# Second attention of a ViT tower: the low half of the probabilities moves from VectorE to GpSimd, ScalarE's high half becomes one operation, and the queues stand in another order

## The chip, the cores and the metric

The kernel runs on one core of a Trainium2 chip. A core has TensorE (PE, matrix products into PSUM), VectorE (DVE), ScalarE (ACT), GpSimd (POOL) and SyncE (SP, which issues DMAs); each works through its own queue in order, and queues meet at semaphores. The metric is the time of one execution on the device in microseconds, the median of several runs. Times inside the kernel come from one profiled execution.

## The reference

64 images go through five steps: patch embedding, a first attention, a first MLP, the second attention, a second MLP. The change is in the second attention. With its 196 patches an image is one frame, so both parts of the reference's formula are plain attention over all 197 tokens of 192 channels, with 12 heads of 64:

```python
def _L1_attn_ref(x, W_qkv, W_0):            # x: normalised tokens, 64 x 197 x 192
    def _mhsa(q, k, v, scale):
        s = jnp.einsum('ghid,ghjd->ghij', q, k) * scale
        a = jax.nn.softmax(s, axis=-1)
        return jnp.einsum('ghij,ghjd->ghid', a, v)
    ...
    qkv = (x @ W_qkv).reshape(b, t, dh, 3, h)
    ...
    out = jnp.concatenate((out_cls, out_sp), axis=2)
    out = jnp.transpose(out, (0, 2, 1, 3)).reshape(b, t, h * dh)
    return out @ W_0
h = h + _L1_attn_ref(_layernorm(h, axis=-1), L1_attn_W_qkv, L1_attn_W_0)
```

Everything is float32 there. The kernel computes such products with float16 pairs: a number is split into a high part (its rounding to float16) and a low part (the rest), and three of the four partial products are summed.

## The kernel before, in words

The residual `h` of all images stays in SBUF. `attention_1` handles one image in each round of a loop, written out for an even and an odd image. An image has 197 tokens, in two row blocks of 128 and 69 (index `c`), and six pairs of heads (`n`). Each engine has a list of steps, its order. A step has a letter and a number; an apostrophe means that it belongs to the next image (two: to the one after), a caret to the image before. The lists set each engine's order fully; nothing is scheduled at run time but the waits.

The steps of one image, in the order of the data:
- `n`: VectorE normalises the image (`normalise_twice`, L137 and L139: two instructions for each row block, SBUF to SBUF, float32).
- `x`: TensorE transposes it into a bank (L1266, L1267), ScalarE copies the high part (L1334), VectorE subtracts for the low part (L1402, tile `fp`).
- `q0` to `q5`, `v0` to `v3`: TensorE makes queries and keys of a pair (L1273, ten matmuls) or half of the values of a row block (L1280, five); ScalarE takes the high part (L1348, L1334), VectorE the low one (L1419, L1402). The steps `x`, `q`, `v` and `w` share two PSUM banks in turn (`JOBS`, `job_before`), so each waits until VectorE has emptied the bank of the job before the last.
- `s`: TensorE's scores of a pair (L1291). `m` of VectorE: their maxima (L1429). `e` of ScalarE: four exponentials with their sums (L1363, into `b_pr`, three buffers). `r`: VectorE's reciprocal of the sums (L1435). `p` of GpSimd: two multiplications by it, in `b_pr` (L1512).
- `h`: ScalarE's high part of the probabilities (L1334, `b_halves`, two instructions, one for each row block). `l`: their low part, a subtraction with two SBUF inputs, for each row block. Pairs 2 and 5 have it on GpSimd (L1497), the others on VectorE (L1402).
- SyncE transposes both halves by DMA (L1478). `m` of TensorE: probabilities times values (L1305). `o`: output in two halves (L1334, L1402). `w`: output projection (L1315) and VectorE's addition to `h` with its statistics (L1454, L1458); in odd images two row blocks more than in even ones. `k`: GpSimd lays aside the left-over tokens of odd images (L1505).

Exponential `n` needs low part `n - 3` finished, high part `n` needs the DMA of `n - 3`, reciprocal `n` needs multiplication `n - 2`.

Of the kernel before, what the change touches and what calls it, by code (L numbers as in the profile page):

```python
# [1084 lines left out]
def attention_1(nc, S, n_img):  # L1085
# [9 lines left out]
    VH = 2 * D  # L1095
    FLIP_ROWS = (P, TAIL + 11)
    QUERIES = sum(FLIP_ROWS)
    PE_ORDER = ("m5^^ v2 s5^ q5 w^^ s0 x' v3 m0^ s1 m1^ m2^ q0' s2 q1' q2' m3^ s3 "
                "v0' q3' m4^ s4 q4' v1'").split()
    ACT_ORDER = ("e2 v0' q3' o1^ e3 q4' h1 v1' o2^ h2 v2' e4 q5' e5 h3 h4 v3' x'' "  # L1100
                 "e0' o0 h5 q0'' e1' q1'' q2'' h0'").split()
    DVE_ORDER = ("v1 o2^^ v2 m5^ r4^ n' q5 w^^ r5^ l3^ m0 v3 x' l4^ r0 m1 q0' o0^ m2 "
                 "r1 q1' q2' l0 m3 v0' r2 q3' m4 o1^ r3 q4' l1").split()
    POOL_ORDER = ("p1 p2 l2 p3 k^ p4 p5 p0' l5").split()
    JOBS = [s for s in PE_ORDER if s[0] in "xqvw"]
    assert len(JOBS) % 2 == 0

# [27 lines left out]
    with ExitStack() as ctx:  # L1135
# [91 lines left out]
        with nc.Block() as block:  # L1227
# [101 lines left out]
            @block.scalar  # L1329
            def _(act):  # L1330
                norm_s(act)

                def copy(dst, src):
                    return nc.scalar.activation(dst, src, ACT.Copy)  # L1334

                def step(s, kind, n, img, like, odd):
                    if kind in "xqv":
                        k = job_bank(kind, n)
                        act.wait_ge(*made(s, img))
                    if kind == "x":  # L1340
                        if later(img):
                            act.wait_ge(q_ready, PAIRS * img)
                            act.wait_ge(v_ready, 4 * img)
                        copy(xt[:, 0:2], banks[:, k, 0:2 * SEQ].rearrange("p (h t) -> p h t", h=2)).then_inc(xt_hi, 1)
                    elif kind == "q":
                        if later(img):
                            act.wait_ge(ready, PAIRS * (img - 1) + n + 1)
                        nc.scalar.activation(qk[:, n, 0], banks[:, k, 0:2 * SEQ].rearrange("p (g t) -> p g t", g=2), ACT.Copy,  # L1348
                                             scale=QK_SCALE).then_inc(qk_hi, 1)
                    elif kind == "v":  # L1350
                        if n % 2 == 0 and later(PAIRS * (img - 2) + 3):
                            act.wait_ge(mixed, PAIRS * (img - 2) + 3 * (n // 2) + 3)
                        c, col = n % 2, (n // 2) * VH
                        copy(val[odd][0:ROWS[c], 0, c, col:col + VH], banks[0:ROWS[c], k, 0:VH]).then_inc(v_hi, 1)
                    elif kind == "e":
                        if later(PAIRS * img + n - 1):
                            act.wait_ge(inverted, PAIRS * img + n - 1)
                        if later(PAIRS * img + n - 2):
                            act.wait_ge(*low_made(img, n - 3, 1))
                        for e in range(2):  # L1360
                            act.wait_ge(max_made[e], PAIRS * img + n + 1)
                            for c in range(2):
                                last = nc.scalar.activation(pr[n % 3][0:ROWS[c], c, e, :], scores[n % 2][0:ROWS[c], e, c * SEQ:(c + 1) * SEQ],  # L1363
                                                            ACT.Exp, bias=nmx[n % 2][0:ROWS[c], c, e:e + 1],
                                                            accum_out=rsum[n % 2][0:ROWS[c], c, e:e + 1])
                            last.then_inc(freed[e], 1)
                        if isinstance(img, int) and img == n_img - 1 and n in (2, 3):
                            gather_left(n - 2)
                    elif kind == "h":
                        act.wait_ge(prob_made, PAIRS * img + n + 1)  # L1370
                        if later(PAIRS * img + n - 2):
                            act.wait_ge(*turned(img, n - 3))
                        for c in range(2):
                            copy(halves[n % 3][0:ROWS[c], c, 0, :, 0:SEQ], pr[n % 3][0:ROWS[c], c]).then_inc(high_made, 1)
                    elif kind == "o":
                        act.wait_ge(mixed, PAIRS * img + 2 * n + 2)
                        if n == 0 and later(img - odd):
                            act.wait_ge(w_ready, img - odd)
                        if n == 0 and odd and later(img - 1):
                            act.wait_ge(left_taken, img - 1)  # L1380
                        copy(ot[:, 0, 2 * n:2 * n + 2, own(odd)], bank_o[:, (odd + n) % 2, 0:2 * SEQ].rearrange("p (f t) -> p f t", f=2)).then_inc(ot_hi, 1)

                def gather_left(m):
                    pairs = range(n_img // 2)[m * LEFT_PAIRS:(m + 1) * LEFT_PAIRS]
                    act.wait_ge(left_taken, 2 * pairs[-1] + 2)
                    copy(gathered[m].rearrange("p k (i t) -> p k i t", t=REST),
                         ol[:, 2 * pairs[0] + 1:2 * pairs[-1] + 2:2, :].rearrange("p i (k t) -> p k i t", t=REST)).then_inc(left_gathered, 1)

                run(act, ACT_ORDER, step)
                gather_left(2)  # L1390

            @block.vector
            def _(dve):
# [10 lines left out]
                def step(s, kind, n, img, like, odd):  # L1404
# [26 lines left out]
                    elif kind == "r":  # L1431
                        if later(PAIRS * img + n - 1):
                            dve.wait_ge(prob_made, PAIRS * img + n - 1)
                        dve.wait_ge(freed[1], PAIRS * img + n + 1)
                        v.reciprocal(rinv[n % 2][:], rsum[n % 2][:]).then_inc(inverted, 1)  # L1435
                    elif kind == "l":
                        for c in range(2):
                            dve.wait_ge(high_made, 2 * (PAIRS * img + n) + c + 1)
                            low(halves[n % 3][0:ROWS[c], c, 1, :, 0:SEQ], pr[n % 3][0:ROWS[c], c],
                                halves[n % 3][0:ROWS[c], c, 0, :, 0:SEQ]).then_inc(low_by_v, 1)  # L1440
                    elif kind == "o":
                        dve.wait_ge(ot_hi, 3 * img + n + 1)
                        low(ot[:, 1, 2 * n:2 * n + 2, own(odd)], bank_o[:, (odd + n) % 2, 0:2 * SEQ].rearrange("p (f t) -> p f t", f=2),
                            ot[:, 0, 2 * n:2 * n + 2, own(odd)]).then_inc(ot_split, 1)
                    elif kind == "w":
                        if isinstance(img, int) and img == 0:
                            dve.wait_ge(moved, 16 * MOVES)
                        if isinstance(img, int) and img == n_img - 1:
                            add_left(0, banks[:, 1 - k, 0:D])
                            add_left(1, banks[:, 1 - k, D:2 * D])  # L1450
                        dve.wait_ge(*made(s, img))
                        tiles = ((img - 1, 1), (img, 0)) if odd else ((img, 0),)
                        for m, (i, c) in enumerate(tiles):
                            last = v.tensor_tensor(h[:, i, c, :], banks[:, k, m * D:(m + 1) * D], h[:, i, c, :], ALU.add)  # L1454
                        last.then_inc(h_updated, 1)
                        dve.wait_ge(h_updated, img + 1)
                        for i, c in tiles:
                            v.bn_stats(S["stats"][:, 2 * i + c, :], h[:, i, c, :])  # L1458
# [26 lines left out]
            @block.gpsimd  # L1485
            def _(pool):
                for r in range(3):
                    last = nc.gpsimd.memset(halves[r][:], 0.0)
                last.then_inc(cleared, 1)
                pool.wait_ge(cleared, 1)  # L1490
                pool.wait_ge(filled, 1)

                def step(s, kind, n, img, like, odd):
                    if kind == "l":
                        for c in range(2):
                            pool.wait_ge(high_made, 2 * (PAIRS * img + n) + c + 1)
                            nc.gpsimd.tensor_tensor(halves[n % 3][0:ROWS[c], c, 1, :, 0:SEQ], pr[n % 3][0:ROWS[c], c],  # L1497
                                                    halves[n % 3][0:ROWS[c], c, 0, :, 0:SEQ], ALU.subtract).then_inc(low_by_p, 1)
                        return
# [316 lines left out]
```

## Time and profile before

| | |
|---|---|
| three runs, median | 2526.62 us (2522.15 to 2528.86) |
| profiled execution | 2526.39 us, span of its instructions 2524.6 us |
| busy over the span | PE 2210.4 (88%), DVE 2187.8 (87%), ACT 2067.5 (82%), POOL 1362.8 (54%) |
| granted TensorE clock, mean | 0.971 |
| second attention | from about 790 to 2300 us |
| largest group | L1512 POOL `b_pr`, 768 instructions, 687.1 us busy |

The chain that ended last lies in the last stage only, so it says nothing of the second attention; there the windows, the waits and the timelines have to be read. In a timeline a row merges equal neighbours ("x2"); its duration runs from the first start to the last end. Neighbours overlap by 0.04 to 0.13 us, so what an instruction costs its engine is the difference of two starts, not its duration.

### The profile page before, as it was taken

How to read it: one execution, taken by the hardware profiler on the slowest of the kernel's cores; microseconds unless marked ns; L12 is line 12 of the kernel's file. 1: busy time of each engine (PE TensorE's matmuls, PEld its weight loads, DVE VectorE, ACT ScalarE, POOL GpSimd, SP SyncE). 2: the span in 40 equal slices, each digit the busy share in tenths (PEclk: the TensorE clock that was granted, in tenths of full speed). 3: DMA queues.
4: the chain of work that ended last, by engine and by line, in shares of the span. 5: the costliest groups of instructions: out<-in, count | busy, mean ns of one | idle time of the engine just before them, and what ended most of it. 6: DMA issues, size and time to landing. Idle time of an engine off the chain costs nothing. (4 is left out here: it accounts for less than half of the span.)

```text
span 2524.6 us, 77423 instructions
## 1 busy us (share of the span) xinstructions
PE 2210.4 (88%) x25422; PEld 1717.7 (68%) x25422; DVE 2187.8 (87%) x5350; ACT 2067.5 (82%) x6129; POOL 1362.8 (54%) x1778
## 2 busy tenths in 40 slices
PE   5899999999998888888888888888898888888876
PEld 5778876888786666666666666666666666665554
DVE  5776668888885999999999999999999999996876
ACT  4677776777773898889888988988898889886997
POOL 5777742333331566656565666666565666662322
PEclk9999999999999999999999999999999999997999
DMA  6344410001000765556555555655565556562111
GB/s 179 107 114 121 117 30 28 5 5 42 14 5 3 110 116 108 112 111 114 109 108 108 112 113 107 115 109 112 110 115 108 110 110 115 112 111 47 53 46 57
DMA packets 734157, 222.65 MB, mean 88 GB/s; under 512 B 667590, under 2 KB 732720, under 8 KB 733808
## 3 DMA queue, kind: packets, MB, share of 16 engines
q1 hardware_dynamic: 734064, 221.56, 42.9%
q8 instruction: 41, 0.67, 0.1%
q14 instruction: 52, 0.43, 0.1%
HBM read 46.49 MB, written 9.68 MB: 22 GB/s over the span
## 5 line engine op out<-in xcount | busy, mean ns | idle before, releaser
L1512 POOL TENSOR_TENSOR b_pr<-b_pr,fc 128x394 f32<-128x394 f32 (+1 forms) x768 | 687.1, 917 | 453.7 <-DVE fc L1435 453.5
L1363 ACT ACTIVATE b_pr<-b_scores,fc 128x197 f32<-128x197 f32 (+1 forms) x1536 | 632.1, 439 | 43.3 <-DVE fc L1429 42.2
L1273 PE MATMUL b_banks<-fp,wqkv 128*128 128x197 f16 x3840 | 392.0, 250 | 65.1 <-DVE fp L1402 47.7
L1273 PEld LDWEIGHTS b_banks<-fp,wqkv 128*128 128x128 f16 x3840 | 315.2, 98 | 127.7 <-DVE fp L1402 56.1
L1429 DVE TENSOR_REDUCE fc<-b_scores 128x2 f32<-128x394 f32 x768 | 396.0, 555 | 2.4 <-PE b_scores L1291 0.4
L1334 ACT ACTIVATE b_halves<-b_pr 128x394 f16<-128x394 f32 (+1 forms) x768 | 367.4, 548 | 3.6 <-DMA b_pt<-b_halves 0.9
L1402 DVE TENSOR_TENSOR b_halves<-b_pr,b_halves 128x394 f16<-128x394 f32 (+1 forms) x512 | 359.2, 743 | 3.6 <-ACT b_halves L1334 1.6
L1363 ACT ACTIVATION_READ_ACCUMULATOR b_pr<-b_scores,fc 128x1 f32 (+1 forms) x1536 | 338.9, 221 | 0.0
L1497 POOL TENSOR_TENSOR b_halves<-b_pr,b_halves 128x394 f16<-128x394 f32 (+1 forms) x256 | 227.8, 912 | 131.8 <-ACT b_halves L1334 131.8
L977 POOL TENSOR_TENSOR h<-h,fp_bias 69x192 f32 (+3 forms) x128 | 133.4, 1070 | 266.8 <-DVE m_xn L139 266.8
L1291 PE MATMUL b_scores<-b_qk 64*128 64x197 f16 (+1 forms) x4608 | 270.5, 251 | 5.7 <-ACT b_pr L1363 5.7
L1280 PE MATMUL b_banks<-wqkv,fp 128*128 128x384 f16 (+1 forms) x1280 | 263.0, 338 | 6.1 <-DVE b_qk L1419 2.2
L479 PE MATMUL tokens<-tok_w,parts 128*128 128x192 f16 (+1 forms) x2304 | 207.8, 251 | 49.9 <-POOL parts L338 49.9
L1291 PEld LDWEIGHTS b_scores<-b_qk 64*128 64x128 f16 (+1 forms) x4608 | 186.4, 104 | 78.8 <-issue 56.9
L479 PEld LDWEIGHTS tokens<-tok_w,parts 128*128 128x128 f16 (+1 forms) x2304 | 194.1, 108 | 60.2 <-POOL parts L338 40.6
L1334 ACT ACTIVATE b_val<-b_banks 128x384 f16<-128x384 f32 (+1 forms) x256 | 126.5, 494 | 111.2 <-PE b_banks L1280 111.2
L1419 DVE SCALAR_TENSOR_TENSOR b_qk<-b_banks,b_qk 128x394 f16<-128x394 f32 x384 | 205.3, 548 | 13.1 <-ACT b_qk L1348 12.9
L338 POOL TENSOR_TENSOR parts<-patches,parts 128x394 f16<-128x394 f32 x192 | 179.0, 962 | 51.5 <-ACT parts L381 51.5
L1348 ACT ACTIVATE b_qk<-b_banks 128x394 f16<-128x394 f32 x384 | 192.1, 507 | 11.5 <-PE b_banks L1273 9.1
L1077 PE MATMUL m_bank_y<-fp,m_hid 128*128 128x192 f16 (+1 forms) x2304 | 195.4, 246 | 1.3 <-DVE h L955 1.3
L1077 PEld LDWEIGHTS m_bank_y<-fp,m_hid 128*128 128x128 f16 (+1 forms) x2304 | 190.4, 105 | 1.7 <-issue 1.5
L1025 ACT ACTIVATE m_act<-m_bank_h,fc_bias 128x394 f32<-128x394 f32 x192 | 112.8, 588 | 87.1 <-PE m_bank_h L1066 75.2
(250 smaller groups left out, 4437.7 us busy)
## 6 DMA issues: line engine op xcount, KB each, us to landing
patches<-in_x SPq DMA_DIRECT2D x64, 588.0 KB, 4.3
b_pt<-b_halves SPq DMA_TRANSPOSE x384, 3.2
out<-z_res SPq DMA_DIRECT2D x64, 96.0 KB
fc<-b_halves SPq DMA_TRANSPOSE x192, 3.2
fp<-b_halves SPq DMA_TRANSPOSE x192, 3.2
m_raw_weights<-in_wqkv SPq DMA_DIRECT2D x2, 1152.0 KB, 6.9
out<-z_res SPq DMA_DIRECT2D x32, 51.8 KB
h<-h SPq DMA_DIRECT2D x32, 44.2 KB
```

Of the source, the lines that this page charges most:

```text
L479: last = t.matmul(tokens[m][0:ROWS[c], c * D:(c + 1) * D], parts[m][:, pa, k, COLS[c]], tok_w[:, pb, k, :], start=(k == 0 and n == 0), sto ...
L1077: last = t.matmul(bank_y[m][0:ROWS[c], c * D:(c + 1) * D], hid[b][:, pa, f, lo:lo + ROWS[c]], S["fp"][:, pb, f, :], start=(f == 0 and j == ...
L1273: last = t.matmul(out[:, g * SEQ:(g + 1) * SEQ], w[:, (2 * n + g) * P:(2 * n + g + 1) * P], x, start=(j == 0), stop=(j == 4))
L1280: last = t.matmul(out[0:ROWS[c], 0:VH], x[:, COLS[c]], w[:, col:col + VH], start=(j == 0), stop=(j == 4))
L1291: last = t.matmul(scores[n % 2][0:ROWS[c], e, c * SEQ:(c + 1) * SEQ], qk[rows, n, pa, 0, COLS[c]], qk[rows, n, pb, 1, :], start=(j == 0), ...
L1334: return nc.scalar.activation(dst, src, ACT.Copy)
L1363: last = nc.scalar.activation(pr[n % 3][0:ROWS[c], c, e, :], scores[n % 2][0:ROWS[c], e, c * SEQ:(c + 1) * SEQ], ACT.Exp, bias=nmx[n % 2][ ...
L1402: return v.tensor_tensor(dst, src, high, ALU.subtract)
L1419: v.scalar_tensor_tensor(out=qk[:, n, 1], in0=banks[:, k, 0:2 * SEQ].rearrange("p (g t) -> p g t", g=2), scalar=QK_SCALE, in1=qk[:, n, 0], ...
L1429: v.reduce_max(nmx[n % 2][:, :, e], scores[n % 2][:, e, 0:2 * SEQ].rearrange("p (c t) -> p c t", c=2), AX.X, negate=True).then_inc(max_mad ...
L1497: nc.gpsimd.tensor_tensor(halves[n % 3][0:ROWS[c], c, 1, :, 0:SEQ], pr[n % 3][0:ROWS[c], c], halves[n % 3][0:ROWS[c], c, 0, :, 0:SEQ], ALU ...
L1512: last = nc.gpsimd.tensor_tensor(p, p, inv, ALU.mult)
```

## The change

1. `POOL_ORDER` has `l` for all six pairs, `DVE_ORDER` none.
2. ScalarE's `h` is one instruction over both row blocks, 128 rows of 2 x 394 elements. For that the rows 69 to 127 of the second block of `b_pr` are set to zero once, at the start, by three GpSimd memsets, and ScalarE's first exponential waits for them. A low part waits for the whole high part, no longer for its row block's half.
3. All four orders are new. Among other things the next image's normalisation is made one image earlier (`n''`), behind reciprocal 4 and ahead of `w` and reciprocal 5.

```diff
-    PE_ORDER = ("m5^^ v2 s5^ q5 w^^ s0 x' v3 m0^ s1 m1^ m2^ q0' s2 q1' q2' m3^ s3 "
-                "v0' q3' m4^ s4 q4' v1'").split()
...
+    PE_ORDER = ("m0^ w^^ v3 s0 x' s1 m1^ m2^ q0' q1' s2 q2' v0' m3^ s3 q3' q4' m4^ "
+                "s4 v1' s5 m5^ q5' v2'").split()
+    ACT_ORDER = ("q2' h0 v0' e2 q3' e3 q4' h1 v1' o1^ o2^ h2 q5' v2' e4 e5 h3 v3' h4 "
+                 "x'' e0' h5 q0'' o0 q1'' e1'").split()
+    DVE_ORDER = ("m0 v3 x' m1 r0 q0' q1' m2 r1 o0^ q2' v0' m3 q3' r2 m4 q4' v1' r3 "
+                 "o1^ o2^ q5' v2' m5 r4 n'' w^ r5").split()
+    POOL_ORDER = ("l5^ l0 k^^ p1 p2 l1 l2 p3 p4 l3 p5 l4 p0'").split()
...
                     elif kind == "e":
+                        if isinstance(img, int) and img == 0 and n == 0:
+                            act.wait_ge(cleared, 1)
...
-                        for c in range(2):
-                            copy(halves[n % 3][0:ROWS[c], c, 0, :, 0:SEQ], pr[n % 3][0:ROWS[c], c]).then_inc(high_made, 1)
+                        copy(halves[n % 3][:, :, 0, :, 0:SEQ], pr[n % 3][:]).then_inc(high_made, 1)
...
                 for r in range(3):
+                    last = nc.gpsimd.memset(pr[r][:, 1], 0.0)
+                last.then_inc(cleared, 1)
+                for r in range(3):
                     last = nc.gpsimd.memset(halves[r][:], 0.0)
                 last.then_inc(cleared, 1)
...
                     if kind == "l":
+                        pool.wait_ge(high_made, PAIRS * img + n + 1)
                         for c in range(2):
-                            pool.wait_ge(high_made, 2 * (PAIRS * img + n) + c + 1)
```

VectorE before, from reciprocal 4 to low part 3, in the round ahead of the loop:

```order
L1435 RECIPROCAL fc<-fc 128x4
L137 TENSOR_SCALAR fc<-h,mean,rstd 128x128
L139 TENSOR_SCALAR fc<-h,mean,rstd 128x128
L137 TENSOR_SCALAR fc<-h,mean,rstd 69x128
L139 TENSOR_SCALAR fc<-h,mean,rstd 69x128
L1419 SCALAR_TENSOR_TENSOR b_qk<-b_banks,b_qk 128x394
L1454 TENSOR_TENSOR h<-b_banks,h 128x192
L1458 BN_STATS stats<-h 128x6
L1435 RECIPROCAL fc<-fc 128x4
L1402 TENSOR_TENSOR b_halves<-b_pr,b_halves 128x2x197
L1402 TENSOR_TENSOR b_halves<-b_pr,b_halves 69x2x197
```

VectorE now, the same place, from the maxima of pair 5 to reciprocal 5:

```order
L1430 TENSOR_REDUCE fc<-b_scores 128x2 x2
L1436 RECIPROCAL fc<-fc 128x4
L137 TENSOR_SCALAR fc<-h,mean,rstd 128x128
L139 TENSOR_SCALAR fc<-h,mean,rstd 128x128
L137 TENSOR_SCALAR fc<-h,mean,rstd 69x128
L139 TENSOR_SCALAR fc<-h,mean,rstd 69x128
L1455 TENSOR_TENSOR h<-b_banks,h 128x192
L1459 BN_STATS stats<-h 128x6
L1436 RECIPROCAL fc<-fc 128x4
```

The normalisation still stands between reciprocals 4 and 5, now of the image after the next; the low parts (`b_halves`) behind reciprocal 5 are gone, and a low part of queries and keys (`b_qk`) no longer stands between normalisation and addition.

GpSimd before, multiplications (`b_pr`, with the number of the buffer) 3, 4, 5 and 0 and the low part (`b_halves`) of pair 5:

```order
L1512 TENSOR_TENSOR b_pr0<-b_pr0,fc 128x394
L1512 TENSOR_TENSOR b_pr0<-b_pr0,fc 69x394
L1512 TENSOR_TENSOR b_pr1<-b_pr1,fc 128x394
L1512 TENSOR_TENSOR b_pr1<-b_pr1,fc 69x394
L1512 TENSOR_TENSOR b_pr2<-b_pr2,fc 128x394
L1512 TENSOR_TENSOR b_pr2<-b_pr2,fc 69x394
L1512 TENSOR_TENSOR b_pr0<-b_pr0,fc 128x394
L1512 TENSOR_TENSOR b_pr0<-b_pr0,fc 69x394
L1497 TENSOR_TENSOR b_halves2<-b_pr2,b_halves2 128x2x197
L1497 TENSOR_TENSOR b_halves2<-b_pr2,b_halves2 69x2x197
```

GpSimd now, from multiplication 3 to the low part of pair 4:

```order
L1516 TENSOR_TENSOR b_pr0<-b_pr0,fc 128x394
L1516 TENSOR_TENSOR b_pr0<-b_pr0,fc 69x394
L1516 TENSOR_TENSOR b_pr1<-b_pr1,fc 128x394
L1516 TENSOR_TENSOR b_pr1<-b_pr1,fc 69x394
L1501 TENSOR_TENSOR b_halves0<-b_pr0,b_halves0 128x2x197
L1501 TENSOR_TENSOR b_halves0<-b_pr0,b_halves0 69x2x197
L1516 TENSOR_TENSOR b_pr2<-b_pr2,fc 128x394
L1516 TENSOR_TENSOR b_pr2<-b_pr2,fc 69x394
L1501 TENSOR_TENSOR b_halves1<-b_pr1,b_halves1 128x2x197
L1501 TENSOR_TENSOR b_halves1<-b_pr1,b_halves1 69x2x197
```

Between two multiplications there is now a low part, and multiplication 5, which needs reciprocal 5, comes behind low part 3.

## Rows read from the trace of the kernel before

**Rows 1.** Window sums, 300 us of the second attention; stretch, length, busy by engine, PEclk, DMA.
```profile
1200.00:1500.00 300.00, 264.06 (x3306) 201.28 (x3306) 288.57 (x622) 265.40 (x958) 184.55 (x213) 0.97 0.58 110
```
**Rows 2.** Groups by shape, VectorE, 1200 to 2000 us; count, busy us, mean ns, idle.
```profile
L1402 DVE TENSOR_TENSOR b_halves<-b_pr,b_halves 69x394 f16<-69x394 f32 x139 | 123.1, 885 | 0.0
...
L1402 DVE TENSOR_TENSOR b_halves<-b_pr,b_halves 128x394 f16<-128x394 f32 x139 | 82.8, 596 | 1.1
...
L137 DVE TENSOR_SCALAR fc<-h,mean,rstd 128x128 f32 x34 | 43.5, 1278 | 4.1 <-issue 2.6
...
L1435 DVE RECIPROCAL fc<-fc 128x4 f32<-128x4 f32 x208 | 34.4, 165 | 4.8 <-ACT b_pr L1363 3.0
...
L137 DVE TENSOR_SCALAR fc<-h,mean,rstd 69x128 f32 x34 | 20.6, 605 | 0.0
```
**Rows 3.** Waits, 1200 to 2000 us: who waited for whom, us in total, times, longest.
```profile
POOL b_pr L1512 <- DVE fc L1435: 236.6, 105, 2.6
POOL b_halves L1497 <- ACT b_halves L1334: 69.3, 34, 2.2
...
PE b_banks L1266 <- DVE b_qk L1419: 59.0, 35, 2.5
ACT b_val L1334 <- PE b_banks L1280: 58.6, 35, 2.7
```
**Rows 4.** Timeline of VectorE: start, us, engine and operation, count, idle before.
```profile
1406.21 0.18 DVE L1435 RECIPROCAL fc<-fc 128x4 f32<-128x4 f32 x1 [0.17 <-ACT b_pr L1363]
1406.47 1.57 DVE L137 TENSOR_SCALAR fc<-h,mean,rstd 128x128 f32 x1
1407.96 0.88 DVE L139 TENSOR_SCALAR fc<-h,mean,rstd 128x128 f32 x1
1408.77 0.33 DVE L137 TENSOR_SCALAR fc<-h,mean,rstd 69x128 f32 x1
...
1409.28 0.55 DVE L1419 SCALAR_TENSOR_TENSOR b_qk<-b_banks,b_qk 128x394 f16<-128x394 f32 x1
1409.76 0.34 DVE L1454 TENSOR_TENSOR h<-b_banks,h 128x192 f32 x1
```
**Rows 5.** Timeline of GpSimd, from 1405 us.
```profile
1405.51 3.25 POOL L1512 TENSOR_TENSOR b_pr<-b_pr,fc 128x394 f32<-128x394 f32 x4
...
1417.20 1.78 POOL L1497 TENSOR_TENSOR b_halves<-b_pr,b_halves 128x394 f16<-128x394 f32 x2
1418.93 2.05 POOL L1512 TENSOR_TENSOR b_pr<-b_pr,fc 128x394 f32<-128x394 f32 x2
```
**Rows 6.** Timeline of ScalarE, from 1418 us.
```profile
1418.23 0.94 ACT L1348 ACTIVATE b_qk<-b_banks 128x394 f16<-128x394 f32 x2
1419.07 0.94 ACT L1334 ACTIVATE b_halves<-b_pr 128x394 f16<-128x394 f32 x2
1419.91 0.41 ACT L1363 ACTIVATE b_pr<-b_scores,fc 128x197 f32<-128x197 f32 x1
...
1421.51 0.49 ACT L1334 ACTIVATE b_val<-b_banks 128x384 f16<-128x384 f32 x1
1421.88 0.50 ACT L1348 ACTIVATE b_qk<-b_banks 128x394 f16<-128x394 f32 x1
1422.26 0.51 ACT L1334 ACTIVATE b_ot<-b_bank_o 128x394 f16<-128x394 f32 x1
```
**Rows 7.** Groups by shape, ScalarE, whole span; a wide copy of the first stage.
```profile
L381 ACT ACTIVATE parts<-patches 128x1182 f16<-128x1182 f32 x64 | 76.2, 1191 | 91.5 <-PE tokens L479 91.2 <-DMA patches<-in_x 0.2
```
**Rows 8.** Timeline of TensorE, from 1409 us.
```profile
1409.96 0.32 PE L1266 MATMUL b_banks<-ident,fc 128*128 128x128 f32 x1 [2.47 <-DVE b_qk L1419]
...
1410.36 1.03 PE L1280 MATMUL b_banks<-wqkv,fp 128*69 128x384 f16 x5
```
**Rows 9.** Window sums, columns as in rows 1.
```profile
1412.00:1414.00 2.00, 2.00 (x26) 1.40 (x22) 1.99 (x6) 1.45 (x7) 0.98 (x1) 0.50 0.77 148
```

More of the change, by code:

```diff
@@ L1097, in attention_1 @@
     QUERIES = sum(FLIP_ROWS)
-    PE_ORDER = ("m5^^ v2 s5^ q5 w^^ s0 x' v3 m0^ s1 m1^ m2^ q0' s2 q1' q2' m3^ s3 "
-                "v0' q3' m4^ s4 q4' v1'").split()
[L1100 to L1104, printed above, removed]
+    PE_ORDER = ("m0^ w^^ v3 s0 x' s1 m1^ m2^ q0' q1' s2 q2' v0' m3^ s3 q3' q4' m4^ "
[5 more added lines that the diff above has]
+    POOL_ORDER = ("l5^ l0 k^^ p1 p2 l1 l2 p3 p4 l3 p5 l4 p0'").split()
     JOBS = [s for s in PE_ORDER if s[0] in "xqvw"]
@@ L1436, in step @@
                     elif kind == "l":
+                        dve.wait_ge(high_made, PAIRS * img + n + 1)
                         for c in range(2):
-                            dve.wait_ge(high_made, 2 * (PAIRS * img + n) + c + 1)
                             low(halves[n % 3][0:ROWS[c], c, 1, :, 0:SEQ], pr[n % 3][0:ROWS[c], c],
@@ L1487, in _ @@
                 for r in range(3):
+                    last = nc.gpsimd.memset(pr[r][:, 1], 0.0)
+                last.then_inc(cleared, 1)
+                for r in range(3):
                     last = nc.gpsimd.memset(halves[r][:], 0.0)
                 last.then_inc(cleared, 1)
-                pool.wait_ge(cleared, 1)
+                pool.wait_ge(cleared, 2)
                 pool.wait_ge(filled, 1)
```

## Prediction

> **What bounds the kernel now.** I read the window sums first, to see which engine has no room in the second attention. There VectorE (DVE) is busy 96% of the time, ScalarE (ACT) and TensorE (PE) 88%, GpSimd (POOL) 62% [rows 1]. Then the groups by shape, for counts: 208 reciprocals, one for each pair of heads, in 800 us are 34.67 images, so one image takes 23.08 us [rows 2]. Then the waits: GpSimd is idle 236.6 us until a reciprocal of VectorE and 69.3 us until a high part of ScalarE, ScalarE 58.6 us until TensorE's value product, TensorE 59.0 us until VectorE has emptied a bank for the next image's transposes [rows 3]. All of them end, directly or one step on, at VectorE's queue. So an image costs what VectorE's queue costs: 288.57 / 300 x 23.08 = 22.2 us of work and 0.9 of idle time.
>
> Last the timelines, to see why VectorE's instructions are long. A low part of the probabilities should take 0.48 us for each of its two instructions; it takes 596 and 885 ns in the mean [rows 2]. The normalisation of the next image is four instructions, of which the first and third take 1278 and 605 ns in the mean, though one alone can take 0.33 [rows 2, 4]. Set the two timelines side by side. GpSimd ran four multiplications back to back from 1405.51 to 1408.76, at a pace of 0.80 ((3.25 - 0.04) / 4), so the second ended at 1407.15 and the third at 1407.95. VectorE's normalising instruction of 1406.47 ended at 1408.04, the next at 1408.84: each about 0.08 us behind the end of a GpSimd instruction. Once GpSimd had stopped, the last two took 1408.77 to 1409.28 = 0.51 together [rows 4, 5]. So whatever of VectorE reads only SBUF queues behind GpSimd, the first of a block even past two ends.
>
> **What is removed.** Four of six low parts leave VectorE: 139 of each shape in 34.67 images, so four pairs an image, (82.8 + 123.1) / 34.67 = 5.9 us by busy time, some 5.3 from start to start, since neighbours overlap by 0.08 [rows 2]. VectorE's sum falls from 22.2 to 16.9, plus what normalising gains below, so about 18. It is not the bound by its sum any more.
>
> **What GpSimd gets.** A multiplication pair takes 2 x 0.80 = 1.60; a low part 1417.20 to 1418.93 = 1.73 [rows 5]. Six of each are 20.0 us an image, with the copy of the left tokens 20.2. That is a floor: no less than 20.2 of 23.08.
>
> The Trainium skill (GPSIMD Engine Reference, section Key points) says VectorE is about twice as fast for elementwise work. By that rule alone the move is a loss: four pairs at 1.73 instead of 0.95 are 3.1 us more engine time an image. It decides only if GpSimd then is the last engine, which the sum above does not make it.
>
> **ScalarE's high part.** Two instructions take 1419.07 to 1419.91 = 0.84 now [rows 6]. The new one has 788 elements a row; the trace of this stage has none such. Bounds: not below one half (0.42), not above both (0.84). Between: 1182 elements of the same kind of copy take 1.191 us [rows 7], 394 take 0.52, so 0.85 ns an element and 0.86 for 788, less the 0.10 that neighbours overlap: 0.76. Taken: 0.76, a gain of 0.5 us an image. The price is that the low part waits for all of it, and not for its first half; that delay, 0.34, is hidden where GpSimd still multiplies.
>
> **The order.** Now find the chain that closes on itself. In the new queues the next image's normalisation stands behind reciprocal 4 and ahead of the residual addition and reciprocal 5 (the pieces of the order in the part on the change). TensorE's transposes need both: the normalised image, and the bank that the addition frees. ScalarE's copy of them heads the rest of its round. So a round is the path: ScalarE from that copy to exponential 4; VectorE from reciprocal 4 over the normalisation to the addition; TensorE's transposes; back to ScalarE. Its legs:
>
> ScalarE: five exponentials at 1.60 (1419.91 to 1421.51) = 8.00; four high parts at 0.76 = 3.04; six query-key copies at 0.40 (between 0.42, two from 1418.23 to 1419.07, and 0.38, from 1421.88 to 1422.26) = 2.40; three value copies at 0.37 = 1.11; three output copies and the transposes' copy, all of 394 elements, at 0.38 = 1.52 [rows 6]. Sum 16.07. Exponential 5, two high parts and a value copy stand beside VectorE's leg: 1.60 + 1.52 + 0.37 = 3.5, less than that leg, so they cost nothing; they would if it fell below 3.5.
>
> VectorE and TensorE: reciprocal 4 and its hand-overs 0.26 (1406.21 to 1406.47). Normalisation: between 3.2 (four ends of GpSimd at 0.80) and 3.9 (first 1.49, then three at 0.80), since GpSimd now has work queued all the while: it is in multiplications 3 and 4 and low part 3; I take 3.6, for it will at times wait for a high part. Before it was 2.81. The addition 0.34, two of them in odd images, mean 0.47; hand-over 0.13 (1409.83 to 1409.96); transposes 0.40 and their tail, 0.60; hand-over 0.10 [rows 4, 8]. Sum 0.26 + 3.6 + 0.47 + 0.13 + 0.60 + 0.10 = 5.16.
>
> ScalarE's waits inside its leg: now it is idle 34.6 us of 300, 2.7 an image [rows 1], 1.7 of it for the value product [rows 3], which in the new order lies outside the leg. That leaves 1.0; bounds 0 and 2.7. I take 1.1, because four operations of the new order (query-key copies 0 and 1, output copy 2, value copy 2) come straight behind the matmuls that make their input.
>
> An image: 16.07 + 5.16 + 1.1 = 22.33 us, 0.75 less than 23.08. Over 62 of 64 rounds, without filling and draining, 46 us. GpSimd is then busy 20.2 / 22.3 = 90%. The new memsets, three of half the width of the probabilities, stand ahead of the stage's first exponential; the first transposes, projections and maxima cover them. The profiled execution took 2526.39 (span 2524.6); the median of the runs is 2526.62, so both bases agree. 2526.4 - 46 = 2480.
>
> **A price of TensorE's clock.** TensorE stood idle 2.47 us before the transposes at 1409.96, and in the stretch from 1412 its granted clock was 0.50 [rows 8, 9]: 1.2 of 2.4 GHz. In the new order it waits at the same place, for VectorE. If all of transposes and the first projection ran at half clock in every image, the path would grow by 0.4 + 0.4; in the sum above this is left at what even images pay now.
>
> **Rivals.**
> First, normalising starves. For: the first instruction of a block already runs past one end of GpSimd that it could have used (1407.15) [rows 4, 5], and GpSimd has hardly a gap any more. Against: the second took exactly one end, and the last two none, with GpSimd at rest. If two more of the four skip an end, normalisation is 3.9 + 1.6 = 5.5, the image 24.2, 1.15 more than now: 62 x 1.15 = 71 and thus about 2598. The point from which it decides is a normalisation of 3.6 + 0.75 = 4.35 us. The Trainium skill (GPSIMD Engine Reference, section Key points) names this contention: GpSimd shares its SBUF interfaces with VectorE's two-port modes and two-SBUF-input instructions. The trace agrees, with 885 and 1278 ns [rows 2]; by that rule the low parts' half of it goes and the normalisation's stays.
> Second, GpSimd is the bound alone. Where GpSimd waits, normalisation takes 4 x 0.26 = 1.04 (0.51 for two [rows 4]) instead of 3.6, and the path falls to 19.8, below GpSimd's 20.2. With about 0.9 of remaining waits for high parts and reciprocal 5: 21.1 an image, 2.0 less, 2526 - 124 = 2402. Against: normalisation lies just where GpSimd has most queued.
> Third, the order eats the gain: ScalarE's waits inside its leg stay at 2.7 instead of 1.1: 16.07 + 5.16 + 2.7 = 23.9 at worst; half of the way there is 23.1, no change, 2526. For: five queues that hand over at many places; against: VectorE, which most waits ended at, has 4 us of room.
>
> **Chances.** Forecast 0.58, with a range of its own from 2450 to 2512 (normalisation 3.2 to 3.9, high part 0.72 to 0.84, waits 0.9 to 1.3). GpSimd alone 0.16. No change 0.09. Starved normalisation 0.17. The range of 8 in 10 cuts the far parts of the first and second rival: 2436 to 2545. A change below 0.3%, 7.6 us, can't be told from none; faster by more 0.75, same 0.09, slower 0.16.
>
> **What would show it.** The reciprocals' count in a window of this stage gives the image: 22.3. The four normalising groups should sum to some 3.6 from start to start; the high part one instruction of some 0.86; VectorE about 80% busy and GpSimd 90%; ScalarE's largest wait the one for the transposes (some 1.6 an image), and GpSimd's waits small. I am wrong if GpSimd's largest wait is still a reciprocal with several us an image, if the normalising mean passes 1.1 us an instruction, or if TensorE's clock falls in every image.

## The result: 2560.8 us, slower, and the profile after

The changed kernel takes 2560.81 us in the median (2560.11 to 2562.59), before 2527.71 in the same rounds: ratio 1.0136, 95% interval 1.0119 to 1.0154. I had forecast 2480.

The page of the changed kernel gives a span of 2558.2 us, and a granted clock of 0.947 against 0.971. The lost time lies in the second attention. Window sums (stretch, length, busy time of PE, weight loads, DVE, ACT and POOL with the number of instructions, PEclk, DMA), answering [rows 1]:

```profile
1200.00:1500.00 300.00, 262.48 (x3224) 207.03 (x3223) 243.59 (x509) 253.84 (x858) 258.01 (x312) 0.93 0.57 107
```

VectorE is down to 81% and GpSimd up to 86%, about as forecast; ScalarE has fallen to 85%, and the clock from 0.97 to 0.93. Groups by shape on VectorE, 1200 to 2000 us (count, busy us, mean ns), answering [rows 2]:

```profile
L137 DVE TENSOR_SCALAR fc<-h,mean,rstd 128x128 f32 x34 | 51.3, 1510 | 3.0
L139 DVE TENSOR_SCALAR fc<-h,mean,rstd 128x128 f32 x34 | 45.1, 1328 | 0.0
...
L1436 DVE RECIPROCAL fc<-fc 128x4 f32<-128x4 f32 x202 | 34.5, 171 | 11.5 <-ACT b_pr L1365 8.2
L137 DVE TENSOR_SCALAR fc<-h,mean,rstd 69x128 f32 x34 | 32.1, 943 | 0.0
L139 DVE TENSOR_SCALAR fc<-h,mean,rstd 69x128 f32 x34 | 21.2, 624 | 0.0
```

202 reciprocals where there were 208: 23.8 us an image by this count, against 23.08. The four normalising instructions sum to (51.3 + 45.1 + 32.1 + 21.2) / 34 = 4.4 us, 4.1 from start to start, where I had 3.6. The waits, answering [rows 3]:

```profile
PE b_banks L1266 <- DVE h L1455: 90.3, 34, 3.4
...
ACT fp L1334 <- PE b_banks L1267: 77.6, 34, 2.7
POOL b_halves L1501 <- ACT b_halves L1334: 53.3, 33, 3.0
POOL b_pr L1516 <- DVE fc L1436: 52.3, 51, 1.6
ACT b_qk L1348 <- PE b_banks L1273: 39.9, 48, 2.0
```

GpSimd's waits have gone from 306 to 106 us. What waits now is TensorE, 90.3 us for the addition behind the normalisation, then ScalarE, 77.6 for the transposes (2.3 us a round, 1.6 forecast) and 39.9 for query-key products: the path of the forecast. VectorE, with a fifth of its time free, also waits 87.7 us for ScalarE's query-key high parts. One round of it, in the timelines of VectorE, GpSimd, TensorE and ScalarE (start, us, instruction, count, idle before), answering [rows 4 to 6] and [rows 8]:

```profile
1419.50 0.18 DVE L1436 RECIPROCAL fc<-fc 128x4 f32<-128x4 f32 x1
1419.77 1.55 DVE L137 TENSOR_SCALAR fc<-h,mean,rstd 128x128 f32 x1
1421.24 1.78 DVE L139 TENSOR_SCALAR fc<-h,mean,rstd 128x128 f32 x1
1422.94 0.92 DVE L137 TENSOR_SCALAR fc<-h,mean,rstd 69x128 f32 x1
1423.78 0.33 DVE L139 TENSOR_SCALAR fc<-h,mean,rstd 69x128 f32 x1
1424.04 0.34 DVE L1455 TENSOR_TENSOR h<-b_banks,h 128x192 f32 x1
...
1443.30 1.47 DVE L137 TENSOR_SCALAR fc<-h,mean,rstd 128x128 f32 x1
```
```profile
1418.80 3.25 POOL L1516 TENSOR_TENSOR b_pr<-b_pr,fc 128x394 f32<-128x394 f32 x4
1422.00 1.78 POOL L1501 TENSOR_TENSOR b_halves<-b_pr,b_halves 128x394 f16<-128x394 f32 x2
1425.07 1.64 POOL L1516 TENSOR_TENSOR b_pr<-b_pr,fc 128x394 f32<-128x394 f32 x2 [1.28 <-DVE fc L1436]
```
```profile
1420.43 0.69 PE L1291 MATMUL b_scores<-b_qk 64*128 64x197 f16 x12
1424.51 0.47 PE L1266 MATMUL b_banks<-ident,fc 128*128 128x128 f32 x1 [3.40 <-DVE h L1455]
1424.78 0.42 PE L1267 MATMUL b_banks<-ident,fc 128*128 128x128 f32 x1
1424.99 0.32 PE L1266 MATMUL b_banks<-ident,fc 69*128 69x69 f32 x1
1425.11 0.32 PE L1267 MATMUL b_banks<-ident,fc 69*128 69x69 f32 x1
1425.36 1.17 PE L1291 MATMUL b_scores<-b_qk 64*128 64x197 f16 x12
1426.46 1.21 PE L1305 MATMUL b_bank_o<-fp,b_val 128*64 128x197 f16 x12
1427.45 0.85 PE L1305 MATMUL b_bank_o<-b_pt,b_val 128*64 128x197 f16 x12
...
1430.06 0.69 PE L1291 MATMUL b_scores<-b_qk 64*128 64x197 f16 x12
```
```profile
1425.62 0.50 ACT L1334 ACTIVATE fp<-b_banks 128x394 f16<-128x394 f32 x1 [2.68 <-PE b_banks L1267]
...
1427.62 0.86 ACT L1334 ACTIVATE b_halves<-b_pr 128x788 f16<-128x788 f32 x1
1429.31 0.50 ACT L1348 ACTIVATE b_qk<-b_banks 128x394 f16<-128x394 f32 x1 [0.82 <-PE b_banks L1273]
```

GpSimd runs without a gap from 1418.80 to 1423.78. The first normalising instruction passes the end at 1420.4 and gets through at 1421.32; the second, 1.78 us long, also lets one end pass (1422.0); the third ends 0.08 behind GpSimd's last; only the fourth takes 0.33. Then TensorE, after 3.40 us idle, runs in this round its transposes and scores at half speed: the twelve score matmuls take 1.17 us, against 0.69 at 1430.06. So does the first product with the values (1.21), and the second in part (0.85; in experiment 2 they take 0.70 and 0.68). The clock in that stretch:

```profile
1424.00:1428.00 4.00, 3.49 (x38) 3.05 (x40) 3.62 (x11) 2.38 (x10) 2.93 (x4) 0.57 0.56 107
```

ScalarE gets the query-key product late and is idle 0.82 us more. From normalisation to normalisation: 4.74 to the transposes, 1.11 to ScalarE's copy, 17.68 to the next block, 23.53.

Not every round is like this one. TensorE's wait ahead of the transposes alternates between 1.9 and 3.4 us. In 10 of the 34 rounds between 1200 and 2000 us all that follows the wait runs at full speed, and from ScalarE's copy to the next block it takes 17.23 us. In the other 24 the half clock begins at the transposes or up to three groups of matmuls later, and the same leg takes 17.7 to 19.3 us. The longest have it through the next twenty query-key matmuls, which then take 3.1 us instead of 1.87.

### The profile page after: what moved, and what is told of

Read it like the earlier page. It is cut to its first block and busy times, and to the rows that moved or that the text cites. A ratio compares the mean times of both kernels' runs of the same rounds, so it can differ in the third digit from the quotient of the medians.

```text
span 2558.2 us, 76264 instructions
## 1 busy us (share of the span) xinstructions
PE 2243.8 (88%) x25422; PEld 1780.4 (70%) x25422; DVE 1979.2 (77%) x4838; ACT 2036.8 (80%) x5745; POOL 1749.3 (68%) x2293
## 5 line engine op out<-in xcount | busy, mean ns | idle before, releaser
L1501 POOL TENSOR_TENSOR b_halves<-b_pr,b_halves 128x394 f16<-128x394 f32 (+1 forms) x768 | 682.3, 910 | 116.6 <-ACT b_halves L1334 105.8
L1516 POOL TENSOR_TENSOR b_pr<-b_pr,fc 128x394 f32<-128x394 f32 (+1 forms) x768 | 626.0, 842 | 116.4 <-DVE fc L1436 116.4
L1273 PE MATMUL b_banks<-fp,wqkv 128*128 128x197 f16 x3840 | 406.2, 262 | 14.0 <-DVE fp L1403 12.7
L1273 PEld LDWEIGHTS b_banks<-fp,wqkv 128*128 128x128 f16 x3840 | 341.2, 103 | 66.3 <-DVE b_val L1403 15.8
L1420 DVE SCALAR_TENSOR_TENSOR b_qk<-b_banks,b_qk 128x394 f16<-128x394 f32 x384 | 217.2, 566 | 167.8 <-ACT b_qk L1348 167.8
L1334 ACT ACTIVATE b_halves<-b_pr 128x788 f16<-128x788 f32 x384 | 340.4, 886 | 3.2 <-POOL b_pr L1516 2.4
L1365 ACT ACTIVATION_READ_ACCUMULATOR b_pr<-b_scores,fc 128x1 f32 (+1 forms) x1536 | 330.2, 215 | 0.0
L1280 PE MATMUL b_banks<-wqkv,fp 128*128 128x384 f16 (+1 forms) x1280 | 251.5, 327 | 2.3 <-DVE b_val L1403 1.7
L1266 PE MATMUL b_banks<-ident,fc 128*128 128x128 f32 (+1 forms) x128 | 36.9, 308 | 168.6 <-DVE h L1455 162.4
L1403 DVE TENSOR_TENSOR b_val<-b_banks,b_val 128x384 f16<-128x384 f32 (+1 forms) x256 | 141.4, 552 | 54.3 <-ACT b_val L1334 54.3
```

Source lines behind the costliest of these rows:

```text
L1273: last = t.matmul(out[:, g * SEQ:(g + 1) * SEQ], w[:, (2 * n + g) * P:(2 * n + g + 1) * P], x, start=(j == 0), stop=(j == 4))
L1280: last = t.matmul(out[0:ROWS[c], 0:VH], x[:, COLS[c]], w[:, col:col + VH], start=(j == 0), stop=(j == 4))
L1420: v.scalar_tensor_tensor(out=qk[:, n, 1], in0=banks[:, k, 0:2 * SEQ].rearrange("p (g t) -> p g t", g=2), scalar=QK_SCALE, in1=qk[:, n, 0], ...
L1516: last = nc.gpsimd.tensor_tensor(p, p, inv, ALU.mult)
```

## The experiments

Times are medians, ratios against the kernel before of the same rounds. "Image" is 800 us divided by a sixth of the reciprocals counted in it; legs are means of the starts over all rounds between 1200 and 2000 us.

### 1. Normalisation ahead of reciprocal 4

```diff
-    DVE_ORDER = "... m5 r4 n'' w^ r5"
+    DVE_ORDER = "... m5 n'' r4 w^ r5"
```

> The changed kernel with one step moved in VectorE's order: the normalisation n'' stands ahead of reciprocal 4, not behind it. Theory A (a round is the closed path normalisation, transposes, ScalarE's copy of them, five exponentials, normalisation): it starts some 0.5 us earlier, and since GpSimd then has no reciprocal 4 to go on with, it meets one multiplication pair only and takes 2.2 to 2.8 us instead of 4.1. The image falls from 23.6 to 21.8 to 22.3 us: 2440 to 2480 us. Theory B (GpSimd at 86% is the bound, so each wait of GpSimd costs): GpSimd now waits some 1.5 us more for reciprocal 4, the image grows to 24.5 or more: 2600 us and above.

Measured: 2401.11 us, ratio 0.9504 (0.9483 to 0.9525), faster than both. Windows, VectorE, GpSimd:

```profile
1200.00:2000.00 800.00, 735.96 (x9673) 574.72 (x9670) 633.00 (x1519) 752.65 (x2579) 768.15 (x930) 1.00 0.65 121
```
```profile
1417.72 0.42 DVE L137 TENSOR_SCALAR fc<-h,mean,rstd 128x128 f32 x1
1418.07 0.88 DVE L139 TENSOR_SCALAR fc<-h,mean,rstd 128x128 f32 x1
1418.87 0.33 DVE L137 TENSOR_SCALAR fc<-h,mean,rstd 69x128 f32 x1
1419.13 0.33 DVE L139 TENSOR_SCALAR fc<-h,mean,rstd 69x128 f32 x1
1419.38 0.16 DVE L1436 RECIPROCAL fc<-fc 128x4 f32<-128x4 f32 x1
```
```profile
1417.22 1.65 POOL L1516 TENSOR_TENSOR b_pr<-b_pr,fc 128x394 f32<-128x394 f32 x2
1419.62 1.64 POOL L1516 TENSOR_TENSOR b_pr<-b_pr,fc 128x394 f32<-128x394 f32 x2 [0.76 <-DVE fc L1436]
```

GpSimd has one multiplication pair, then nothing until reciprocal 4; one normalising instruction waits, 0.88, the other three do not. The block is 1.66 us. GpSimd loses 0.76 there and is still 96% busy; the clock is 1.00. Theory A's path is right, but the time lies below its range, since the block and the clock gain more than it had: image 21.05 us. Theory B is out.

### 2. TensorE kept working ahead of the transposes

```diff
+                    if kind == "x":
+                        if later(PAIRS * (img - 1)):
+                            for e in range(2):
+                                pe.wait_ge(freed[e], PAIRS * (img - 1))
+                        work(12, scores[1][:, 0])
```

> The changed kernel with 12 added matmuls of 394 columns (some 2.0 us) in TensorE's idle time ahead of the next image's transposes, into a scores bank that is free by then; their result is not used. They add nothing to any other engine. Theory C (the half clock after the long idle time costs about 0.8 of the 1.3 us that the image came out above the forecast: transposes, scores and query-key matmuls at half speed, and ScalarE waiting for them): granted clock in the second attention from 0.93 to above 0.98, image 22.8 us, 2505 to 2520 us. Theory D (the clock is a companion, all is in the normalisation): the clock rises and the time stays within 8 us of 2561.

Measured: 2504.31 us, ratio 0.9910 (0.9890 to 0.9930).

```profile
1200.00:2000.00 800.00, 753.44 (x9422) 574.77 (x9423) 675.35 (x1414) 709.90 (x2403) 716.47 (x866) 1.00 0.60 113
```

Theory C holds: clock 1.00, 56 us gained, while the normalising groups keep their times (1491 and 1340 ns for the 128-row ones). ScalarE's leg falls from 18.11 to 17.23 us, the one from transposes to its copy from 0.86 to 0.74. ScalarE's wait for query-key products, 39.9 us in the changed kernel, is 9.0 here.

### 3. Half of the normalisation

```diff
-                            last = normalise_twice(...)
+                            if c == 0 or (isinstance(img, int) and img == 0):
+                                last = normalise_twice(...)
```

> The changed kernel without the normalisation of the second row block (two of four instructions, from the second image on; the output of those rows is of stale values). Theory A (closed path over the normalisation): the block shrinks from 4.09 to some 2.7 us, the image by 1.4 us or, with less idle time and so less half clock, up to 1.9: 2440 to 2475 us. Theory B (GpSimd is the bound): GpSimd has the same work, the time falls by 10 us at most: 2550 or above.

Measured: 2430.92 us, ratio 0.9618 (0.9600 to 0.9637). The block is 2.75 us to its last end instead of 4.17, the image 21.6, the clock 0.97: 2.1 us shorter for 1.4 us of block. Theory A has the direction and named less half clock as the reason for more than 1.4, but the time lies 9 us below its range. GpSimd had the same work, so theory B is out again.

### 4. The high part in two instructions

```diff
-                        copy(halves[n % 3][:, :, 0, :, 0:SEQ], pr[n % 3][:]).then_inc(high_made, 1)
+                        for c in range(2):
+                            copy(halves[n % 3][0:ROWS[c], c, 0, :, 0:SEQ], pr[n % 3][0:ROWS[c], c]).then_inc(high_made, 1)
```

> The changed kernel with ScalarE's high part again in two instructions, and the low part waiting for its row block's half, as before the change. Theory A: ScalarE's leg of the path has four high parts, 4 x 0.09 = 0.36 us more: 22 us more, 2575 to 2590. Theory E (the low part's wait for the whole high part is what costs: GpSimd waits 53 us in 800 for high parts): GpSimd's wait falls by about 0.4 us at each of its waiting places and the time falls, 2530 to 2545.

Measured: 2539.85 us, ratio 1.0054 (1.0034 to 1.0074), so 21 us faster than the changed kernel. Theory E has the size, my sign was wrong: in this order the fused high part costs. I can't say by which hand-over; the wait of GpSimd for high parts fell only from 53.3 to 41.3 us in 800, and the block and the clock moved as well (0.93 to 0.95). By legs, 0.25 of the 0.3 us that a round gets shorter lie between the block's start and ScalarE's copy. The block's first two instructions take 1179 and 1772 ns there, instead of 1510 and 1328.

### 5. The kernel before, only the low parts moved

```diff
-    DVE_ORDER = "... r5^ l3^ m0 v3 x' l4^ r0 ... q2' l0 m3 ... q4' l1"
-    POOL_ORDER = "p1 p2 l2 p3 k^ p4 p5 p0' l5"
+    DVE_ORDER = "... r5^ m0 v3 x' r0 ... q2' m3 ... q4'"
+    POOL_ORDER = "l5^ l0 p1 p2 l1 l2 p3 k^ p4 l3 p5 l4 p0'"
```

> The kernel before with only the low parts moved: all six on GpSimd, in the order l5^ l0 p1 p2 l1 l2 p3 k^ p4 l3 p5 l4 p0'; VectorE's other steps, TensorE's and ScalarE's order and the two-instruction high part as before. Theory A (VectorE loses 5.3 us of work, but its normalisation, behind reciprocal 4 and now beside a GpSimd that always has work queued, grows to some 4 us, and the orders written for two low parts on GpSimd make it wait for high parts): 2520 to 2580 us. Theory F (the move pays by itself, the reordering only spoils it): GpSimd above 90% busy, 2400 to 2450 us.

Measured: 2578.76 us, ratio 1.0203 (1.0182 to 1.0225). Normalising groups of 69 rows:

```profile
L139 DVE TENSOR_SCALAR fc<-h,mean,rstd 69x128 f32 x33 | 44.8, 1357 | 0.0
L137 DVE TENSOR_SCALAR fc<-h,mean,rstd 69x128 f32 x33 | 42.9, 1300 | 0.0
```

Before, L139 took 332 ns and L137 605: now GpSimd does not stop under them. The 128-row ones got shorter (905 and 589 ns, before 1278 and 882), and the whole block went from 2.87 to 3.93 us. The time is in theory A's range, at its upper end. Theory F is out: the move alone loses, and the new orders with the fused high part win back 18 us of it.

### 6. The kernel before, normalisation ahead of reciprocal 4

```diff
-    DVE_ORDER = "v1 o2^^ v2 m5^ r4^ n' q5 ..."
+    DVE_ORDER = "v1 o2^^ v2 m5^ n' r4^ q5 ..."
```

> The kernel before with one step moved: normalisation ahead of reciprocal 4 (m5^ n' r4^ instead of m5^ r4^ n'). Theory A (the place of the normalisation against the reciprocal that sets GpSimd off is what counts, whoever makes the low parts): the block falls from 2.79 to about 1.7 us; VectorE is 96% busy, so the image gets 0.8 to 1.1 us shorter: 2455 to 2480 us. Theory G (the gain in the changed kernel came from its closed path, which this kernel has not): reciprocal 4 is later, GpSimd and ScalarE behind it too, and the time is 2515 us or more.

Measured: 2472.93 us, ratio 0.9786 (0.9769 to 0.9804). Windows, and the group that was 1278 ns:

```profile
1200.00:2000.00 800.00, 710.47 (x9167) 542.07 (x9165) 779.61 (x1727) 736.95 (x2661) 506.78 (x593) 1.00 0.61 115
```
```profile
L137 DVE TENSOR_SCALAR fc<-h,mean,rstd 128x128 f32 x36 | 17.5, 485 | 0.0
```

Theory A, in its range. The same exchange of two steps gains 2.1% with the low parts on VectorE and 6.2% (2401 against 2561) with all of them on GpSimd. So all else of the change is worth 72 us (2473 to 2401) once the normalisation is out of GpSimd's way.

### 7. and 8. From experiment 1 on: high part split, and low part 4 back on VectorE

> The changed kernel with the normalisation ahead of reciprocal 4 (2401 us, GpSimd 96% busy, ScalarE 94%), and the high part again in two instructions with the low part waiting for its half. ScalarE gets 6 x 0.09 = 0.54 us more work an image. Theory H (here GpSimd is the bound and its 0.8 us of waits are for reciprocals): no gain from the earlier low part, and ScalarE's 94% rises to 97%: 2400 to 2425. Theory E (the earlier start of the low parts gains as in the changed kernel): 2380 to 2393.

> The changed kernel with the normalisation ahead of reciprocal 4, and pair 4's low part back on VectorE, behind the maxima of the next image's pair 1. GpSimd loses 1.73 us of 20.2 an image. Theory H (GpSimd's sum is the bound): ScalarE is next with 19.8 us of work, the image falls from 21.1 to some 20.4: 2355 to 2380 us. Theory I (low parts on VectorE and GpSimd's instructions hold each other up, 1.3 us instead of 0.95 for a pair and as much on GpSimd, and ScalarE's queue follows): 2395 to 2430 us.

The edits are that of experiment 4, and `m1 l4^ r0` in VectorE's order with `l4` taken out of GpSimd's. Measured: 2410.90 us, ratio 0.9549 (0.9531 to 0.9567), theory H; and 2400.60, ratio 0.9502 (0.9486 to 0.9518), the same as experiment 1. There GpSimd falls from 96% to 88%, ScalarE stays at 94%, and GpSimd's wait for reciprocals grows from 28.9 to 69.7 us in 800. So GpSimd's sum was not the bound of experiment 1 by itself. What is, stays open; ScalarE's queue, as full in both, is the nearest candidate. Theory I's time came out, but not its reason: VectorE's two instructions took 603 and 556 ns, GpSimd's multiplications 0.85 us at most between 1200 and 2000 us, and nothing but the waits grew.

### 9. Normalisation behind the addition

```diff
-    DVE_ORDER = "... m5 r4 n'' w^ r5"
+    DVE_ORDER = "... m5 r4 w^ n'' r5"
```

> The changed kernel with the normalisation behind the residual addition (m5 r4 w^ n'' r5). Of the two things that the transposes need, the bank then is free early and the normalised image comes last, at about the same time as now. Theory A (the normalisation itself, wherever it stands behind reciprocal 4, closes the path; its instructions meet GpSimd's back-to-back work): the block stays at about 4 us, the image within 0.3 us of 23.6, 2545 to 2585 us. Theory J (the addition behind the block, by freeing the bank late, is what held TensorE): 2500 to 2530.

Measured: 2568.53 us, ratio 1.0153 (1.0113 to 1.0193). VectorE and GpSimd:

```profile
1421.67 0.18 DVE L1436 RECIPROCAL fc<-fc 128x4 f32<-128x4 f32 x1
...
1422.82 0.68 DVE L137 TENSOR_SCALAR fc<-h,mean,rstd 128x128 f32 x1
1423.41 1.77 DVE L139 TENSOR_SCALAR fc<-h,mean,rstd 128x128 f32 x1
1425.11 0.92 DVE L137 TENSOR_SCALAR fc<-h,mean,rstd 69x128 f32 x1
1425.95 0.33 DVE L139 TENSOR_SCALAR fc<-h,mean,rstd 69x128 f32 x1
```
```profile
1420.96 3.25 POOL L1516 TENSOR_TENSOR b_pr<-b_pr,fc 128x394 f32<-128x394 f32 x4
1424.17 1.78 POOL L1501 TENSOR_TENSOR b_halves<-b_pr,b_halves 128x394 f16<-128x394 f32 x2
1426.45 1.64 POOL L1516 TENSOR_TENSOR b_pr<-b_pr,fc 128x394 f32<-128x394 f32 x2 [0.50 <-DVE fc L1436]
```

The time is theory A's, the block is not: it starts later and is 2.6 us long in the mean, 3.46 in this round and 1.70 in every other one. But from reciprocal 4 to its last end it takes 4.61 us here and 4.78 in the other rounds, in the changed kernel 4.60 and 4.27. Here it ends behind the end of GpSimd's run at 1425.95, which from multiplication 3 to low part 3 is 5 us of released work. In the other rounds the addition ahead of it first waits 1.57 us for TensorE's output projection, and the last two instructions again come behind the end of GpSimd's run. Theory J is out. The block's end, not its length, is what counts; GpSimd alone does not set it.

### 10. The kernel before, TensorE kept working

The edit of experiment 2 in the kernel before, with `work(6, ...)`.

> The kernel before with 6 added matmuls of 394 columns (1.0 us) ahead of the transposes, as a control for the clock: there VectorE's queue is 96% busy and sets the image, and the half clock comes in every other image only. Theory C (the clock costs where TensorE's work stands in a closed path, and little where VectorE is the bound): the granted clock rises from 0.97 to above 0.99 and the time stays within 10 us of 2527. Theory K (the half clock costs the same in any order): 15 to 30 us faster.

Measured: 2515.89 us, ratio 0.9963 (0.9949 to 0.9977): some 9 us, with the clock at 1.00. Theory C, though at the edge of its bound (the interval is 6 to 13 us); VectorE stays 97% busy. In the kernel before, the half clock comes in only 11 of 35 rounds between 1200 and 2000 us.

## Why the prediction was wrong

- **The path** was right: block, addition, transposes, ScalarE's copy, ScalarE's queue. Experiments 1 and 3 shorten the block and the image with it; in 9 the block's end stays, and so does the time. Its legs were forecast at 4.90 and 17.43 us (0.26 of reciprocal 4 in the second); they are 5.55 and 18.11, image 23.7. That is 0.65 and 0.68 too much, 62 x 1.33 = 82 us.
- **The clock** is the step that failed. I named the half clock, priced transposes and first projection at 0.8 us, and left the sum "at what even images pay now". But the wait at that place grew from (59.0 us in 35 times) 1.7 to (90.3 in 34) 2.7 us, and the half clock now comes in 24 of 34 rounds. It does not stop at the first products: it also takes in scores, products with the values and query-key products, with ScalarE behind them, up to 2.0 us of ScalarE's leg in a round. Experiment 2 measures it: 56 of the 81 us that were missing.
- **The normalisation** was mis-sized: 3.6 taken, 4.1 measured, 0.5 x 62 = 31 us. In half of the rounds the second instruction skips an end of GpSimd as well, the rival of starving in its mild form; its point of decision, 4.35, was not reached, and the block alone would have left a gain: 2504 with the clock kept.
- The two together, 56 + 31, are 87 and not 81 us. They don't add up exactly, since the 56 are counted against a full clock in every round, and the sum had some half clock in it; the clock kept, ScalarE's leg is 17.23, 0.2 below the forecast.
- **"Whatever of VectorE reads only SBUF queues behind GpSimd"** was too wide: the reciprocals read only SBUF too, and none between 1200 and 2000 us took more than 0.18 us, before or after.
- **GpSimd's floor**, 20.2 us, was not reached: experiment 1 stands at 21.05. Its 2401 is the time that I gave the second rival, and its block meets GpSimd at rest, as I had it there. But GpSimd was not the bound alone, as experiment 8 shows, so the equal number is in part luck.
- **The high part** takes 0.886 us (0.86 forecast), but splitting it again is 21 us faster in the changed kernel and 10 us slower in experiment 1. "Hidden where GpSimd still multiplies" does not hold in the first.
- **The memsets** were not tried alone, but the trace bounds them: they take 0.43 to 0.50 us each and start between 786.7 and 787.4 us, and the first exponential comes at 814.1, before the change at 813.1. From the first to the last exponential it is 1503 us instead of 1469, so the loss lies in the rounds.
- **The image of the normalisation** is not another one, as the part on the change has it. Counted from reciprocal 4 it is the one two ahead in both kernels (`r4^ n'` and `r4 n''`); in both traces two blocks stand ahead of the first reciprocal and the third stands behind reciprocal 4 of the first image (827.65 us before, 828.76 now).
- The Trainium skill (GPSIMD Engine Reference, section Key points) says that GpSimd shares its SBUF interfaces with VectorE's instructions in a two-port mode or with two SBUF inputs. The traces agree that they contend: 1510 ns in the mean for a normalising instruction that took 0.42 us in experiment 1. In which mode it ran no run shows.

## What to carry to other kernels

Before work is moved to GpSimd, look in a closed path for the VectorE instructions that get longer beside it (here the normalisation, SBUF to SBUF), and put them ahead of the step that releases GpSimd's next work: that exchange alone gained 2% in one kernel and 6% in the other. Where TensorE waits at the same place in each round, price the half clock for all that can follow the wait, not for the first products alone, and check it with idle matmuls. An engine that is set free shows no gain until the path that took its place is known.

## What I had not expected of the hardware

- A normalising instruction takes 0.33 us alone and up to 1.78 beside GpSimd, whose own multiplications keep 0.842 us. It can let an end of GpSimd's instructions pass while the next is queued; why it does so in some rounds and not in others with the same neighbours (0.88 and 1.78 us for the same instruction) stays open.
- With two SBUF inputs on both sides both engines lose: in the kernel before, VectorE's low part takes 885 ns and GpSimd's multiplication up to 1.26 us. In the changed kernel, where VectorE's low parts are gone and the normalisation is still there, no multiplication took more than 0.85.
- 12 matmuls without use in each image, 2 us of TensorE's work, made the kernel 56 us faster.
